# First layer of the routed feed-forward computed in turned form, from copied blocks of the tile's expert, with the second bias on VectorE

## The reference, cut to what matters

```python
def _sublayer(xs, g, b, W1e, b1e, W2e, b2e):
    mu = jnp.mean(xs, axis=-1, keepdims=True)
    var = jnp.mean(jnp.square(xs - mu), axis=-1, keepdims=True)
    h = (xs - mu) * jax.lax.rsqrt(var + EPS) * g + b
    return xs + jax.nn.relu(h @ W1e.T + b1e) @ W2e.T + b2e
...
expert = jnp.argmax(scores, axis=1)
alpha = jax.nn.sigmoid(jnp.sum(feats * centroids[expert], axis=-1, keepdims=True))
y = jnp.einsum('te,etd->td', onehot, ys)
out = alpha * y + (1.0 - alpha) * feats
...
g = _silu(_L0_ffn_ref(xn, ...))
x = x + s * g
```

## Time and profile before

| what | us |
|---|---|
| median of 3 runs | 2690.0 |
| lowest and highest run | 2686.49, 2695.47 |
| profiled execution | 2691.32 |
| its span in the trace | 2689.5 |
| second phase, first norm to last silu | 302.5 to 674.0 |

### The profile page before, as it was taken

One profiled execution on the slowest core, in us unless ns is written; L12 is line 12 of the kernel. 1 busy time (PEld: TensorE's weight loads), 2 busy tenths in 40 slices (PEclk: granted clock), 3 DMA queues, 4 the chain that ended last, 5 costly groups with the idle time before them and its releaser, 6 DMA issues.

```text
span 2689.5 us, 36104 instructions
## 1 busy us (share of the span) xinstructions
PE 2252.5 (84%) x9632; PEld 1219.3 (45%) x9633; DVE 1748.6 (65%) x2951; ACT 924.5 (34%) x2466; POOL 886.6 (33%) x722
## 2 busy tenths in 40 slices
PE   6887499999588898789789888977988898898877
PEld 3443266666334444453444345444434443454444
DVE  5777344443258667775867686587758676865866
ACT  2333133232126224512631361245216323622541
POOL 2113300000164326324532542264154325423531
PEclk9998699999599899999889999988998899989889
DMA  4342500010212102201220221112012102211210
GB/s 144 117 139 68 162 29 27 27 30 26 87 40 76 44 16 61 79 12 36 68 63 1 60 72 36 32 57 77 3 36 75 56 0 65 67 36 32 60 52 8
DMA packets 140003, 146.21 MB, mean 54 GB/s; under 512 B 47025, under 2 KB 99889, under 8 KB 139825
## 3 DMA queue, kind: packets, MB, share of 16 engines
q1 hardware_dynamic: 132530, 131.49, 17.2%
q0 software_dynamic: 3072, 8.41, 1.0%
q10 hardware_dynamic: 4224, 4.19, 0.5%
HBM read 116.48 MB, written 27.43 MB: 54 GB/s over the span
## 4 chain that ended last, share of the span: by engine, by line
issue 26%; PE 24%; DVE 11%; POOL 10%; ACT 2%; DVEq 0%; DMA 0%; POOLq 0%; ACTq 0%
PE bank L1304 14%; DVE arena L1672 3%; DVE arena L1665 3%; POOL arena L1900 3%; POOL arena L1905 3%; DVE arena L1652 3%; PE bank L1220 2%; PE bank L1173 2%; POOL arena L1907 2%; PE bank L1127 1%; ACT arena L1475 1%; PE bank L1200 1%; PE bank L1190 1%; ACT arena L1484 1%; PE bank L1133 1%
## 5 line engine op out<-in xcount | busy, mean ns | idle before, releaser
L1918 POOL TENSOR_TENSOR arena<-arena 128x512 f32<-128x512 f32 x256 | 343.2, 1341 | 587.0 <-DVE arena L1672 574.8
L1127 PE MATMUL bank<-arena 128*128 128x512 f32 (+2 forms) x896 | 443.5, 639 | 39.3 <-ACT arena L1436 18.3
L1304 PE MATMUL bank<-arena 128*128 128x512 f32 (+2 forms) x1312 | 448.5, 497 | 6.3 <-ACT arena L1440 6.3
L1672 DVE TENSOR_TENSOR_SCAN arena<-arena 128x512 f32<-128x512 f32 x256 | 356.4, 1392 | 12.2 <-issue 10.0
L1475 ACT ACTIVATE arena<-bank,arena 128x128 f32<-128x128 f32 (+3 forms) x512 | 266.3, 530 | 247.5 <-DVE arena L1652 247.5
L1304 PEld LDWEIGHTS bank<-arena 128*128 128x128 f32 x1312 | 256.4, 210 | 193.6 <-issue 157.1
L1173 PE MATMUL bank<-arena 64*128 64x128 f32 (+3 forms) x1024 | 223.7, 516 | 129.5 <-ACT arena L1475 119.8
L1127 PEld LDWEIGHTS bank<-arena 128*128 128x128 f32 (+2 forms) x896 | 164.1, 194 | 287.1 <-issue 231.2
L1652 DVE TENSOR_REDUCE arena<-bank 128x2 f32<-128x256 f32 (+3 forms) x256 | 207.5, 811 | 79.9 <-PE bank L1176 79.9
L1484 ACT ACTIVATE arena<-bank 128x128 f32<-128x128 f32 (+3 forms) x512 | 199.6, 442 | 121.0 <-PE bank L1190 120.9
L1190 PE MATMUL bank<-arena 128*128 128x128 f32 x1280 | 208.6, 300 | 36.9 <-ACT arena L1484 29.7
(11 more groups left out here) (201 smaller groups left out, 2963.8 us busy)
## 6 DMA issues: line engine op xcount, KB each, us to landing
arena<-values SPq DMA_DIRECT2D x256, 256.0 KB, 3.4
arena<-in_L_attn_h SPq DMA_DIRECT2D x16, 512.0 KB, 3.5
arena<-in_W1T SPq DMA_DIRECT2D x8, 1024.0 KB, 6.7
arena<-in_W2T SPq DMA_DIRECT2D x8, 1024.0 KB, 10.2
sorted_rows<-arena SPq DMA_DIRECT2D x42, 128.5 KB, 8.9
arena<-sorted_rows SPq DMA_DIRECT2D x40, 128.5 KB, 2.1
gate_rows<-arena SPq DMA_DIRECT2D x39, 128.0 KB, 1.7
s_rows<-arena ACTq DMA_DIRECT2D x8, 512.0 KB, 3.0
```

Of the source, the lines that this page charges most:

```text
L1127: last = nc.tensor.matmul(dst[rows, :], w, x, start=(n == 0), stop=(n == len(pairs) - 1))
L1304: last = nc.tensor.matmul(dst[o], w, x, start=first, stop=last_one)
L1672: nc.vector.tensor_tensor_scan(state[n % STATES][:, 1:T + 1], proj["w"][:, m, :], kv[n % 2], VEC["init"][:, m * HD + j:m * HD + j + 1], AL ...
L1918: nc.gpsimd.tensor_tensor(prods[n % PRODS], state[n % STATES][:, 0:T], proj["r"][:, m, :], ALU.mult).then_inc(prod_done, 1)
```

## The change

- `expand` computes z already turned. The block of W1 is the stationary operand and nT the moving one: for each of the eight blocks of 128 hidden channels two products with 128 columns, sixteen in all, written straight into `zT_bank`, of which there are now two pairs (the banks that z had). `turn_z` and `z_out` are gone, and so are their semaphores.
- The products need W1 at fixed addresses. A new step, `bring`, copies the 2 x 1024 weights of tile k+2's expert into one of two buffers `w1_now`: one half ScalarE, one half VectorE. On VectorE it stands between norm(k+2) and scale_norm(k+2), on ScalarE behind relu(k). TensorE no longer loads the expert's number for expand.
- `hT` has two buffers.
- The product with the row of ones is gone. Instead, SP's queue loads the expert's row of b2, spread over all partitions, for each tile (`load_b2`, four tiles ahead, behind the load of xs), and VectorE adds alpha times it to xs in a new step `base`, between relu(k) and norm(k+2). norm(k+2) also waits for base(k)'s signal.
- `tile_expert` has two more entries, set to zero in `phase_a`, as the loads run past the last tile.

```diff
 def expand(k, u):
-    e = expert_of(pe, k)
     pe.wait_ge(nT_done, k + 1)
+    pe.wait_ge(w1_left, k + 1)
+    pe.wait_ge(w1_right, k + 1)
     for half in range(2):
-        for c in range(KD):
-            last = nc.tensor.matmul(z_bank[half][:, :], nT[u % 2][:, c, :],
-                                    w1s[:, bass.ds(e * (KD * F) + (c * F + half * 512), 512)],
-                                    start=(c == 0), stop=(c == KD - 1))
-    last.then_inc(z_mm, 1)
+        for f in range(4 * half, 4 * half + 4):
+            for c in range(KD):
+                last = nc.tensor.matmul(zT_bank[u % 2][half][:, (f % 4) * P:(f % 4 + 1) * P], w1_now[u % 2][:, c, f * P:(f + 1) * P],
+                                        nT[u % 2][:, c, :], start=(c == 0), stop=(c == KD - 1))
+        last.then_inc(zT_mm, 1)
...
 def back(k, u):
     e = expert_of(pe, k)
     pe.wait_ge(f_done, k + 1)
-    nc.tensor.matmul(out_bank[u % 2][:, 0:D], ones_row, b2[0:1, bass.ds(e * D, D)], start=True, stop=False)
     pe.wait_ge(h_left, k + 1)
     pe.wait_ge(h_right, k + 1)
...
 # TensorE
 def tile(k, u, ahead=2):
-    turn_z(k)
...
 # ScalarE
+def bring(k, u):
+    e = expert_of(act, k)
+    if not (isinstance(k, int) and k < 2):
+        act.wait_ge(zT_mm, 2 * k - 2)
+    nc.scalar.activation(w1_now[u % 2][:, 0, :], w1s[:, bass.ds(e * KD * F, F)], ACT.Copy).then_inc(w1_left, 1)
 def tile(k, u, ahead=2):
-    relu(k)
-    if ahead >= 1:
-        z_out(k + 1)
+    relu(k, u)
+    if ahead >= 2:
+        bring(k + 2, u + 2)
     silu(k, u)
...
 # VectorE
+def bring(k, u):
+    e = expert_of(v, k)
+    if not (isinstance(k, int) and k < 2):
+        v.wait_ge(zT_mm, 2 * k - 2)
+    nc.vector.tensor_copy(w1_now[u % 2][:, 1, :], w1s[:, bass.ds(e * KD * F + F, F)]).then_inc(w1_right, 1)
+def base(k, u):
+    v.wait_ge(b2_in[u], 4 * k - (4 * u - 16))
+    nc.vector.scalar_tensor_tensor(xs[u][:, 0:D], b2[u], xs[u][:, D:D + 1], xs[u][:, 0:D],
+                                   ALU.mult, ALU.add).then_inc(base_done, 1)
+    v.wait_ge(base_done, k + 1)
 norm(0, 0)
 scale_norm(0, 0)
 norm(1, 1)
-z_out(0)
+v.wait_ge(ffn_loaded, 16 * 2 * E)
+bring(0, 0)
+bring(1, 1)
 scale_norm(1, 1)
 def tile(k, u, ahead=2):
-    relu(k)
+    relu(k, u)
+    base(k, u)
     if ahead >= 2:
         norm(k + 2, u + 2)
-    if ahead >= 1:
-        z_out(k + 1)
-    if ahead >= 2:
+        bring(k + 2, u + 2)
         scale_norm(k + 2, u + 2)
     finish(k, u)
...
 # SP's queue
+def load_b2(k, u):
+    e = expert_of(sp, k)
+    sp.dma_start(b2[u], io["b2row"][:, bass.ds(e * D, D)].broadcast_to([P, D])).then_inc(b2_in[u], 16)
```

More of the change, by code:

```diff
@@ L377, in _ @@
         def _(v):
+            v.memset(tile_expert[:, SLOTS:SLOTS + 2], 0)
             v.memset(zeros, 0.0).then_inc(zeros_set, 1)
@@ L592, in phase_b @@
         nT = [mem.take(KD, P) for _ in range(2)]
-        z_sb = mem.take(F)
-        hT = mem.take(FC, P)
+        w1_now = [mem.take(KD, F) for _ in range(2)]
+        hT = [mem.take(FC, P) for _ in range(2)]
+        b2 = [mem.take(D) for _ in range(RING)]
         f_sb = [mem.take(D) for _ in range(2)]
@@ L598, in phase_b @@
         b1 = mem.take(E * FC)
-        b2 = mem.take(E * D)
-        turn_bank, z_bank, zT_bank, out_bank = bank[0], bank[1:3], bank[3:5], bank[5:7]
+        turn_bank, zT_bank, out_bank = bank[0], (bank[1:3], bank[3:5]), bank[5:7]
         small_in = sem("small_in")
@@ L609, in phase_b @@
         nT_done = sem("nT_done")
[L610 to L613, removed]
+        w1_left = sem("w1_left")
+        w1_right = sem("w1_right")
+        zT_mm = sem("zT_mm")
+        b2_in = [sem(f"b2_in{u}") for u in range(RING)]
+        base_done = sem("base_done")
         h_left = sem("h_left")
@@ L640, in _ @@
                 sp.dma_start(dst, io[name][:, :]).then_inc(small_in, 16)
-            sp.dma_start(b2[0:1, :], io["b2row"][:, :]).then_inc(small_in, 16)
+            def load_b2(k, u):
+                e = expert_of(sp, k)
+                sp.dma_start(b2[u], io["b2row"][:, bass.ds(e * D, D)].broadcast_to([P, D])).then_inc(b2_in[u], 16)
             for k in range(RING):
                 sp.dma_start(xs[k], dram["sorted"][k * P:(k + 1) * P, :]).then_inc(xs_in[k], 16)
+            for k in range(RING):
+                load_b2(k, k)
             for dst, src in loads:
@@ L656, in _ @@
                     sp.dma_start(xs[u], dram["sorted"][bass.ds((k + RING) * P, P), :]).then_inc(xs_in[u], 16)
+                    load_b2(k + RING, u)
             for u in range(REST):
@@ L665, in _ @@
             ident = const[:, 0:P]
-            ones_row = const[0:1, CONST["ones"][0]:CONST["ones"][0] + P]
             def turn_norm(k):
@@ L701, in back @@
                 for c in range(FC):
-                    last = nc.tensor.matmul(out_bank[u % 2][:, 0:D], hT[:, c, :],
-                                            w2s[:, bass.ds((E - 1) * FC * D + c * D - e * (FC * D), D)], start=False, stop=(c == FC - 1))
+                    last = nc.tensor.matmul(out_bank[u % 2][:, 0:D], hT[u % 2][:, c, :],
+                                            w2s[:, bass.ds((E - 1) * FC * D + c * D - e * (FC * D), D)], start=(c == 0), stop=(c == FC - 1))
                 last.then_inc(out_mm, 1)
             pe.wait_ge(ffn_loaded, 16 * 2 * E)
-            pe.wait_ge(small_in, 64)
+            pe.wait_ge(small_in, 48)
             turn_norm(0)
@@ L726, in _, with relu @@
                 act.sem_inc(g_stored[u], 16)
[L728 to L732, removed]
+            def bring(k, u):
                 e = expert_of(act, k)
-                act.wait_ge(z_turned, 2 * k + 1)
+                if not (isinstance(k, int) and k < 2):
+                    act.wait_ge(zT_mm, 2 * k - 2)
+                nc.scalar.activation(w1_now[u % 2][:, 0, :], w1s[:, bass.ds(e * KD * F, F)], ACT.Copy).then_inc(w1_left, 1)
+            def relu(k, u):
+                e = expert_of(act, k)
+                act.wait_ge(zT_mm, 2 * k + 1)
                 for c in range(4):
-                    last = nc.scalar.activation(hT[:, c, :], zT_bank[0][:, c * P:(c + 1) * P], ACT.Relu,
+                    last = nc.scalar.activation(hT[u % 2][:, c, :], zT_bank[u % 2][0][:, c * P:(c + 1) * P], ACT.Relu,
                                                 bias=b1[:, bass.ds(e * FC + c, 1)])
@@ L758, in _ @@
             v.sem_inc(f_done, 2)
-            v.wait_ge(small_in, 64)
+            v.wait_ge(small_in, 48)
             def norm(k, u):
@@ L779, in scale_norm, with relu @@
                 last.then_inc(nT_done, 1)
[L781 to L785, removed]
+            def bring(k, u):
                 e = expert_of(v, k)
-                v.wait_ge(z_turned, 2 * k + 2)
+                if not (isinstance(k, int) and k < 2):
+                    v.wait_ge(zT_mm, 2 * k - 2)
+                nc.vector.tensor_copy(w1_now[u % 2][:, 1, :], w1s[:, bass.ds(e * KD * F + F, F)]).then_inc(w1_right, 1)
+            def relu(k, u):
+                e = expert_of(v, k)
+                v.wait_ge(zT_mm, 2 * k + 2)
                 for c in range(4):
-                    last = nc.vector.tensor_scalar(hT[:, 4 + c, :], zT_bank[1][:, c * P:(c + 1) * P],
+                    last = nc.vector.tensor_scalar(hT[u % 2][:, 4 + c, :], zT_bank[u % 2][1][:, c * P:(c + 1) * P],
                                                    b1[:, bass.ds(e * FC + (4 + c), 1)], 0.0, ALU.add, ALU.max)
@@ L1986, in build @@
         after_pos = mem.at
-        tile_expert = mem.take(SLOTS).bitcast(I32)
+        tile_expert = mem.take(SLOTS + 2).bitcast(I32)
         w_at = mem.at
```

13 lines of the change are left out of this document (4 added, 9 removed).

## The result

| | before | after |
|---|---|---|
| median, us | 2691.4 (4 runs) | 2728.6 (4 runs, 2727.4 to 2730.5) |
| ratio | | 1.0133, 95% interval 1.0116 to 1.0150 |
| span of the profiled execution | 2689.5 | 2725.9 |
| second phase, first turn to end of the last `back` | 368.3 | 402.2 |

What follows compares the result with a forecast made beforehand. The prediction took VectorE's loop through TensorE's turn_norm and back as the bound. Ordinary periods -6.2, branch 0, ends -1.6 and start +1.9 gave -5.9 us: a median of 2684 us, range 2672 to 2699.

Steps and rivals of the forecast that it cites:

- relu after back's end: VectorE, ordinary tile: relu no longer waits for turned z and starts 0.86 us after back's end, instead of 1.06.
- base on VectorE's loop: The new bias step between relu and norm: 0.42 us of work plus 0.08 for its signal, 0.50 in all.
- relu behind a branch tile: VectorE, tile after the loop's branch: counted as ordinary, with relu 0.86 us after back's end.
- L682's load to back: TensorE, from the weight load of turn_norm's turns to back's first product: 0.88 us, where it was 1.41.
- TensorE's pause before the turns: TensorE would idle some 0.9 us a tile in front of turn_norm, waiting for norm's last step on VectorE.
- period, ordinary: Time from one back to the next in an ordinary tile: 8.96 us, against 9.19 before.
- ends: The last two tiles, without a norm ahead: periods shorter by 1.4 and 0.2 us, -1.6 together.
- the signs: Forecast wrong if TensorE's idle time is missing, base or its wait exceeds 0.6, or period is under 8.8 or over 9.2.
- Slower: the granted clock: Rival, chance 0.05: TensorE's new 0.9 us pause per tile lowers its clock to 1.2 GHz; five slow tiles give 2712.
- From turn_norm to back: TensorE's stretch between the turns and back: removing L698's 0.62 us gains 0.53, bounds 0.40 and 0.62.
- At the branch: Every fourth tile, at the loop's branch: relu gains 0, base +0.50, L698's removal -0.53, so no change.
- dear ends: Rival, chance 0.12: VectorE's loop with base 0.70, L698 worth 0.40, no relu gain; +12 us, 2702.

Runs made afterwards that it cites:

- The fillers: Changed kernel plus unread TensorE work in its pauses: products in both 2707.0 us, turns in both 2709.1, a product in the first only 2709.0, second only 2708.9.
- the run of the bias part: Kernel before with b2 loaded per tile and added by base on VectorE, bias product L698 removed, expand, turn_z and z_out kept: 2708.1 us, ratio 1.0031.
- the early-number run: Changed kernel with TensorE loading the expert's number of back(k) ahead of expand(k+1) instead of behind turn_norm(k+2): 2679.1 us, ratio 0.9939.

## Why the prediction was wrong

Point by point, as the prediction put them:

| step | foretold | measured |
|---|---|---|
| spacing of expand's passes | 0.111 us | (3.76 - 0.19) / 31 = 0.115 |
| relu after back's end | 0.86 | 579.97 - 579.14 = 0.83 |
| base on VectorE's loop | 0.50 | 581.63 - 579.97 = 1.66 from relu to norm, 1.04 before: 0.62 |
| relu behind a branch tile | 0.86 | 1.03 (0.98 after the start of finish) |
| base itself | 0.42 | 0.476 |
| L682's load to back | 0.88 | 1.18 |
| TensorE's pause before the turns | 0.9 | 0.88 |
| period, ordinary | 8.96 | 9.35 |
| bring | hidden | hidden, 0.69 on VectorE, 1.06 on ScalarE |
| ends | -1.6 | -1.5 without the slow back |
| granted clock | 1.00 (0.05 for the rival) | 0.94, 23.3 us |

The path at full clock was right: TensorE's work was not the bound, the chain through VectorE was, and TensorE waits where it was said to wait. Even so, two of the signs by which the prediction said that it would be wrong came true: the period is over 9.2, and base with its wait over 0.6. Three things failed.

First and largest, the step "Slower: the granted clock". It gave the clock 0.05, because one pause of 1.45 us was followed by full speed. In the changed kernel two pauses stand close together, 0.88 and 0.75 us with two turns between them, and this comes every tile. The prediction counted only the first: its own figure of 0.88 us from the turns to back held a second pause, and it never stood in the rival. The fillers show the cause: with either pause filled nearly all slow backs go, with both filled, even with turns, all in the loop, and 18 us come back. Its price was wrong too: it took whole tiles at the lower level, some 6 us each (by that figure one such tile eats the gain of 5.9, not two), and the trace has half a back, 1.7 us, fourteen times. That a second pause alone need not be enough stood in the trace before, 2.6 us behind the row of 1.45 and still at a granted clock of 1.00:

```profile
816.17 1.07 PE L1220 MATMUL bank<-arena 128*32 128x512 f32 x8 [0.82 <-ACT arena L1484]
```

No row before had such pauses in every tile, as the prediction said itself.

Second, the term "From turn_norm to back" was mis-sized. L698 was thought to be worth 0.53 of its 0.62 us. It was worth 0.23 here and 0.33 in the run of the bias part. While L698 ran, TensorE's queue did the address arithmetic of back behind it; without L698 this arithmetic stands bare. The bounds, 0.40 and 0.62, missed it; the early-number run shows that the whole 1.18 us was queue but for 0.41. This is 0.3 us a tile, 11 us.

Third, base: 0.62 instead of 0.50, as its signal and the address step behind it cost 0.13 and not 0.08, and it took 0.476 and not 0.42, 4 us. At the branch, and in the tile behind it, the period grew by 0.41; the prediction had nothing at the branch and -0.23 behind it. There relu gains nothing or 0.03, so base's 0.62 less L698's 0.23 stand alone. Without the clock the sum is 10.8 for the nine rounds, -1.5 for the ends and +1.5 for the start (15.3 us from the first turn to the first back before, 16.8 after): +11, near what the kernels with fillers show (2709 against 2695). The "dear ends" rival comes to +12, but by luck: it had base at 0.70, L698 at 0.40 and no gain of relu, and none of the three is what was measured.

In the sum of an ordinary tile the gains of relu (-0.23) and L698 (-0.23) are smaller than the cost of base (+0.62), so the change as a whole had to lose even at full clock. That balance, not the removed work on TensorE, was the question.

What stays open: how long, how close or how frequent pauses must be for the clock to fall, and why some tiles with equal pauses (0.87 and 0.75) have a slow back and others do not: of the 18 tiles of the changed kernel with these pauses six have one.

## What to carry to other kernels

When an engine is busy 96% and another engine's chain arrives just in time, taking work from the first can bring nothing; walk the loop that goes through both, term by term, before pricing what is removed. A short operation can be free or cost all of its length depending on its place in a strict queue (base, 0.56 us a tile), and a register load behind a wait cost 0.35 to 0.77 us a tile on TensorE and some 0.4 on VectorE: load it ahead of the wait. Look at all pauses of TensorE between two dense stretches together, not at the longest one, before trusting its clock; a filler of idle products tells the clock's share in one run.

## What the runs showed of the hardware

- TensorE's granted clock fell to 1.2 GHz for part of 14 of 39 backs behind pauses that were each 0.64 to 1.5 us, 2.0 to 2.8 us from the last pass of expand to the first of back with two turns in between. With the first pause filled the loop kept 2.4 GHz, with the second filled all but two of its backs did. The Trainium skill (TensorE: Matmul & The Clock Gate, Why this matters for your kernels) warns of a long idle gap between bursts; here no single gap was long.
- Turns hold the clock: twelve turns of 128x128 in the pauses did what two products did (0 slow backs, 2709.1 against 2709.0). The Trainium skill (TensorE: Matmul & The Clock Gate, Part 4: PE-mode transpose) says that the transpose mode does not count as busy in the same way; the run does not bear that out for this use.
- Passes of 128 float32 columns with a weight load each run 0.115 us apart, 32 in a row. The eight passes of 512 columns before took 3.44 us, 0.43 each, a quarter of which is 0.108: four times as many weight loads cost at most 0.01 us a pass.
